# Attention to feed-forward: a residual sum earlier on VectorE, and the third pair's rows turned and split earlier

## The chip, the core and the metric

One core of a Trainium2 chip runs the whole program. Its engines are TensorE (PE in the profile; PEld is its weight load), VectorE (DVE), ScalarE (ACT), GpSimd (POOL) and SyncE (SP), each with its own list of instructions in program order, held together by semaphores. The metric is the device time of one execution in microseconds, lower is better; where a kernel has several runs, the median counts.

## What is computed

32 sequences of 128 tokens with 128 features, worked on in 16 pairs. Three blocks follow each other: attention with 16 heads, a feed-forward block, and a graph attention.

```
mod = silu(c) @ W_mod + b_mod
sh_msa, sc_msa, g_msa, sh_mlp, sc_mlp, g_mlp = split(mod, 6)
x = x + g_msa * attention(modulate(layernorm(x), sh_msa, sc_msa))
x = x + g_mlp * ff(modulate(layernorm(x), sh_mlp, sc_mlp))
x = graph_attention(x, c, adj, ...)      # uses sums over adj's last axis, plain and weighted by w_bias
```

ff is `gelu(x @ W1 + b1) @ W2 + b2` with 512 hidden features. Matmul operands are split into a high part (a cast to fp32r) and a low part (the rest), and three products are added up.

## The kernel before

Every phase is a function that writes out, for each engine, the order of its steps by hand. attention_phase walks the 16 pairs; its last pair (LAST, number 15) has a body of its own, last_body, in which the feed-forward block begins for the first pairs: `fed.` calls are steps of ffn_phase, and F0 to F3 are its first four pairs. DONE stands for the step after LAST, in which LAST's output is projected, gated, turned back and summed.

What happens for one pair of the feed-forward block, in order: moments (VectorE, mean and variance), rstd_of (GpSimd), normalise (VectorE, L1671), turn (TensorE, two transposes into PSUM, L1503), modulate (ScalarE, L1607, from PSUM to f_xT in SBUF), split (VectorE: CAST to f_xT_hi, L1685, then the difference f_xT_lo, L1687, a TENSOR_TENSOR whose two inputs lie in SBUF), hidden(F, 0) and hidden(F, 2) (TensorE, L1516 to L1518), gelu (ScalarE), output (TensorE, L1527), gate (ScalarE), turn_back (TensorE, L1536), residual (VectorE, L1695).

The end of the attention for one pair: probs_v (TensorE, L754), save_oT_high and save_oT_low (VectorE, L1119 and L1124; ScalarE L1030 for two of the last), project_out in two halves of 12 matmuls (TensorE, L777 to L779), gate (VectorE: a COPY of four columns, L1135, then two TENSOR_SCALARs, L1140), turn_back (TensorE, L787), residual (VectorE, L1152), and the store of x1 by SyncE. All of a pair's output goes through the PSUM bank "out", which is bank C; residual frees it. In LAST's body turn_p(LAST, 1, 1) is the next to write bank C (tp_o10 in the table LAST_BODY). turn_p (TensorE, L737) turns the probabilities, which GpSimd has scaled (L611).

Beside this run the sums over adj: ScalarE casts the numbers (L315), VectorE sums them (sum_cells, L319), GpSimd multiplies them by w_bias (weigh, L324), VectorE sums again. The last weigh is for pair 15 and waits for sum_cells(15), which stands in last_body's end on VectorE.

The feed-forward block's turn for F2 writes the lower half of bank 2, and project_out(DONE) the upper half of bank 3. turn(F2) waits for normalise(F2) and for modulate(F1).

Of the kernel before, what the change touches and what calls it, by code (L numbers as in the profile page):

```python
# [393 lines left out]
def attention_phase(nc, g, ctx, setup, ffn, graph, edges):  # L394
# [66 lines left out]
    def bank_of(s, name):  # L461
        return dict(uses(s.n) if isinstance(s.n, int) else BODY)[name]
# [36 lines left out]
    def wait_free(eng, s, name):  # L499

        eng.wait_ge(bank_free[bank_of(s, name)], count_to(s, name, True))

    def wait_empty(eng, s, name):

        mine = 0 if name in ("xt0", "xt", "fed") else 1
        zero_wait(eng, bank_free[bank_of(s, name)], count_to(s, name, True) - mine)

    def wait_full(eng, s, name):

        eng.wait_ge(bank_full[bank_of(s, name)], count_to(s, name, False))  # L510

    def unit_of(s, half, b):
        return s.n * 4 + (2 * half + b)
# [7 lines left out]
    def weighted_at(s, half, b):  # L521

        return (step_from(s, 1), f"pv_e{b}") if half else (s, f"pv_o{b}")
# [6 lines left out]
    LAST = Step((PAIRS - 1) // 2, (PAIRS - 1) % 2)  # L530
# [14 lines left out]
    F0, F1, F2, F3 = (Step(n // 2, n % 2) for n in range(4))  # L545
# [124 lines left out]
    def tensor(pe):  # L670
# [69 lines left out]
        def probs_v(s, half, b):  # L740

            if half:
                wait_free(pe, s, f"v1{'ab'[b]}")
            else:
                wait_free(pe, step_from(s, -1), f"v0{'ab'[b]}")
            for grp in range(2):
                wait_free(pe, s, turn_name(half, b, grp))
            at_step, name = weighted_at(s, half, b)
            wait_empty(pe, at_step, name)
            bank = bank_of(at_step, name)  # L750
            for j in range(4):
                for e in range(2):
                    head = 8 * half + 2 * j + e
                    last = pe.matmul(work_ps[bank][64 * e:64 * e + 64, j * T:j * T + T],  # L754
                                     v[:, b, head * DH:head * DH + DH], pT[b][:, 2 * j + e, :],
                                     start=True, stop=True)
            last.then_inc(bank_full[bank], 1)

        def project_out(s, half):

            bank = bank_of(s, "out")
            if half == 0:
                wait_empty(pe, s, "out")
                if at(s, 1):
                    pe.wait_ge(g.kept_loaded, KEPT * 16)
                    pe.wait_ge(w_out_split, 1)
                for b in range(2):
                    at_step, name = weighted_at(step_from(s, -1), 0, b)
                    wait_free(pe, at_step, name)
            else:  # L770
                for b in range(2):
                    at_step, name = weighted_at(step_from(s, -1), 1, b)
                    wait_free(pe, at_step, name)
            dst = work_ps[bank][:, 0:2 * T]
            for c in range(4 * half, 4 * half + 4):
                hi, lo = (t[:, c].rearrange("p b t -> p (b t)") for t in (oT_hi, oT_lo))
                pe.matmul(dst, g.w_out_hi[:, c, :], hi, start=(c == 0), stop=False)  # L777
                pe.matmul(dst, g.w_out_hi[:, c, :], lo, start=False, stop=False)  # L778
                last = pe.matmul(dst, g.w_out_lo[:, c, :], hi, start=False, stop=(c == CHUNKS - 1))  # L779
            if half:  # L780
                last.then_inc(bank_full[bank], 1)
# [79 lines left out]
        def last_body():  # L861

            prev = step_from(LAST, -1)
            fed = ffn.parts["tensor_steps"](pe)
            probs_v(prev, 1, 0)
            probs_v(prev, 1, 1)
            scores(LAST, 1, 0)
            scores(LAST, 1, 1)
            turn_p(LAST, 0, 0)
            fed.wait_split(F0)  # L870
            project_v(LAST, "v1a")
            project_v(LAST, "v1b")
            project_out(LAST, 0)
            turn_p(LAST, 0, 1)
            project_out(LAST, 1)

            pe.wait_ge(g.w1_split, 1)
            pe.wait_ge(exp_done, unit_of(LAST, 1, 0) * 8 + 8)
            fed.hidden(F0, 0)
            probs_v(LAST, 0, 0)  # L880
            probs_v(LAST, 0, 1)
            turn_back(LAST)
            pe.wait_ge(exp_done, unit_of(LAST, 1, 1) * 8 + 8)
            fed.turn(F1, fed.turn_ps(F1))
            fed.hidden(F0, 2)
            turn_p(LAST, 1, 0)
            turn_p(LAST, 1, 1)
            fed.hidden(F1, 0)
            probs_v(LAST, 1, 0)
            probs_v(LAST, 1, 1)  # L890
            fed.hidden(F1, 2)
            project_out(DONE, 0)
            project_out(DONE, 1)
            fed.turn(F2, fed.turn_ps(F2))
            fed.output(F0)
            turn_back(DONE)

# [155 lines left out]
    def vector(dve):  # L1053
# [62 lines left out]
        def save_oT_high(s, half, b):  # L1116
            at_step, name, bank, src = oT_at(s, half, b)
            wait_full(dve, at_step, name)
            dve.tensor_copy(oT_hi[:, 4 * half:4 * half + 4, b, :], src).then_inc(oT_high, 1)  # L1119

        def save_oT_low(s, half, b):
            at_step, name, bank, src = oT_at(s, half, b)
            dve.wait_ge(oT_high, unit_of(s, half, b) + 1)
            dve.tensor_tensor(oT_lo[:, 4 * half:4 * half + 4, b, :], src,  # L1124
                              oT_hi[:, 4 * half:4 * half + 4, b, :].bitcast(F32),
                              ALU.subtract).then_inc(bank_free[bank], 1)
# [6 lines left out]
        def gate(s):  # L1133

            dve.tensor_copy(gate_cols[:], pair_cols(step_from(s, -1), slice(6, 8))).then_inc(gate_cols_ready, 1)  # L1135
            dve.wait_ge(gate_cols_ready, s.n)
            wait_full(dve, s, "out")
            src = work_ps[bank_of(s, "out")]
            for b in range(2):
                last = dve.tensor_scalar(gatedT[:, b, :], src[:, b * T:b * T + T], gate_cols[:, b, 0:1],  # L1140
                                         gate_cols[:, b, 1:2], ALU.mult, ALU.add)
            last.then_inc(gated, 1)

        def residual(s):

            dve.wait_ge(residual_loaded, s.n * 16)
            if not at(s, 1):
                dve.wait_ge(x1_stored, (s.n - 1) * 16)
            dve.wait_ge(turned_back, s.n)
            bank = bank_of(s, "out")  # L1150
            flat = lambda t: t[:].rearrange("p b f -> p (b f)")
            dve.tensor_tensor(flat(x1), work_ps[bank][:, 2 * T:4 * T], flat(x_res),  # L1152
                              ALU.add).then_inc(bank_free[bank], 1)
# [95 lines left out]
        def last_body():  # L1249

            prev = step_from(LAST, -1)
            fed = ffn.parts["vector_steps"](dve)
            save_oT_high(prev, 1, 0)
            save_oT_low(prev, 1, 0)
            save_oT_high(prev, 1, 1)
            invert_sums(LAST, 0, 1)
            row_max(LAST, 1, 0)
            save_oT_low(prev, 1, 1)
            save_turned(LAST, 0, 0)
            row_max(LAST, 1, 1)  # L1260
            fed.moments(F1)
            edges.parts["sum_labels"](dve, PAIRS - 2)
            save_turned(LAST, 0, 1)
            invert_sums(LAST, 1, 0)
            gate(LAST)
            fed.normalise(F1)
            fed.copy_mod_cols(F1)
            invert_sums(LAST, 1, 1)
            save_oT_high(LAST, 0, 0)
            save_oT_low(LAST, 0, 0)  # L1270
            save_oT_high(LAST, 0, 1)
            save_oT_low(LAST, 0, 1)
            residual(LAST)
            fed.split(F1)
            save_turned(LAST, 1, 0)
            save_turned(LAST, 1, 1)
            fed.moments(F2)
            fed.copy_mod_cols(F2)
            save_oT_low(LAST, 1, 0)
            save_oT_low(LAST, 1, 1)  # L1280
            fed.normalise(F2)
            fed.moments(F3)
            fed.copy_gate_cols(F0)
            edges.parts["sum_cells"](dve, PAIRS - 1)
            gate(DONE)
            fed.split(F2)
            residual(DONE)
            fed.normalise(F3)

# [36 lines left out]
def step_from(s, k):  # L1326

    return Step(s.half + (s.par + k) // 2, (s.par + k) % 2)
# [7 lines left out]
def at(s, n):  # L1336

    return isinstance(s.n, int) and s.n == n
# [1230 lines left out]
```

## Time and profile before

| what | value |
|---|---|
| median of 3 runs | 591.07 us (590.46 to 592.23) |
| the profiled execution's own time | 591.09 us |
| its span | 589.5 us |
| TensorE busy | 579.8 us, 98% |
| VectorE busy | 508.2 us, 86% |
| ScalarE busy | 474.7 us, 81% |
| GpSimd busy | 294.0 us, 50% |
| granted TensorE clock | 1.00 (2.4 GHz) |

Busy shares are means over the three blocks. last_body runs from about 371 to 397 us of the span, and the steps that are moved lie between 382 and 396 us. Times in the rows are microseconds from the span's start; a row that joins several instructions has their count behind an x and their joint duration. The number in square brackets is idle time of the engine in front of the row, with what released it. Ends of matmuls are modelled.

### The profile page before, as it was taken

The page shows a single profiled execution, that of the slowest core. Times are in us where ns is not written, and L with a number is a line of the kernel's source. Part 1 is how long each engine was busy: PE and PEld are TensorE (multiplying, and loading weights), DVE is VectorE, ACT ScalarE, POOL GpSimd, SP SyncE. Part 2 cuts the span into 40 slices and gives each one's busy share as a digit, 9 for nine tenths or more (in the row PEclk, how much of TensorE's full clock was granted, in tenths as well). Part 3 has the DMA queues.
Part 4 walks back from the last instruction along what each step waited for, and adds up shares of the span by engine and source line. Part 5 has one row for each costly group of instructions (what it writes and reads, how often), then busy time and mean ns, then how long its engine had stood idle before and what let it go on. Part 6 is the DMA issues. An engine that isn't in the chain of part 4 may idle for free.

```text
span 589.5 us, 17417 instructions
## 1 busy us (share of the span) xinstructions
PE 579.8 (98%) x5600; PEld 534.8 (91%) x5600; DVE 508.2 (86%) x1113; ACT 474.7 (81%) x1733; POOL 294.0 (50%) x355
## 2 busy tenths in 40 slices
PE   8999999999999999999999999999999999999997
PEld 8899899999999999999999999988988899999996
DVE  5899988998998889889888988888886989888886
ACT  4988889789879888897898798977887777777772
POOL 4547435445364355363543543646654565555652
PEclk9999999999999999999999999999999999999999
DMA  8310210211202102102012041023343433444321
GB/s 253 79 42 8 53 44 18 58 32 26 57 0 57 48 9 57 38 19 57 10 47 57 0 108 48 14 72 100 114 144 95 112 104 99 120 117 108 98 73 50
DMA packets 63428, 38.99 MB, mean 66 GB/s; under 512 B 19630, under 2 KB 61214, under 8 KB 63390
## 3 DMA queue, kind: packets, MB, share of 16 engines
q1 hardware_dynamic: 61614, 34.28, 21.9%
q0 software_dynamic: 1632, 4.21, 2.3%
q8 instruction: 21, 0.34, 0.2%
q14 instruction: 17, 0.14, 0.1%
q10 hardware_dynamic: 144, 0.02, 0.0%
HBM read 30.73 MB, written 7.76 MB: 65 GB/s over the span
## 4 chain that ended last, share of the span: by engine, by line
PE 91%; DVE 5%; ACT 2%; issue 1%; DMA 0%; POOL 0%; DVEq 0%; ACTq 0%; POOLq 0%
PE banks L724 10%; PE banks L754 10%; PE banks L737 9%; PE banks L2161 7%; PE banks L692 5%; PE banks L696 5%; PE banks L693 5%; PE banks L2129 4%; PE banks L1527 4%; PE banks L2143 4%; PE banks L777 3%; PE banks L778 2%; PE banks L779 2%; PE banks L708 2%; PE banks L710 2%; PE banks L709 2%
## 5 line engine op out<-in xcount | busy, mean ns | idle before, releaser
L611 POOL TENSOR_TENSOR late_blocks<-late_blocks,p_rsum 128x512 f32<-128x512 f32 x96 | 99.0, 1052 | 158.1 <-DVE p_rsum L1101 158.1
L951 ACT ACTIVATE late_blocks<-banks,neg_max 128x128 f32<-128x128 f32 x384 | 137.3, 404 | 27.8 <-DVE neg_max L1095 27.8
L951 ACT ACTIVATION_READ_ACCUMULATOR late_blocks<-banks,neg_max 128x1 f32 x384 | 94.0, 245 | 0.0
L932 ACT ACTIVATE wide<-banks 128x512 f32<-128x512 f32 x124 | 75.5, 611 | 5.7 <-PE banks L696 4.7
L1095 DVE TENSOR_REDUCE neg_max<-banks 128x8 f32<-128x1024 f32 x64 | 76.6, 1196 | 2.4 <-PE banks L724 2.4
L692 PE MATMUL banks<-xT_hi,w_qkv_hi 128*128 128x256 f32 x256 | 77.4, 302 | 0.0
L696 PE MATMUL banks<-xT_hi,w_qkv_lo 128*128 128x256 f32 x256 | 71.7, 280 | 0.0
L693 PE MATMUL banks<-xT_lo,w_qkv_hi 128*128 128x256 f32 x256 | 71.5, 279 | 0.0
L724 PE MATMUL banks<-wide 64*128 64x128 f32 x1024 | 66.0, 278 | 0.2
L724 PEld LDWEIGHTS banks<-wide 64*128 64x128 f32 x1024 | 59.7, 188 | 6.1 <-issue 3.7
L951 ACT ACTIVATE third_p<-banks,neg_max 128x128 f32<-128x128 f32 x128 | 46.9, 387 | 20.5 <-DVE neg_max L1095 20.5
L1119 DVE CAST oT_hi<-banks 128x512 fp32r<-128x512 f32 x62 | 42.5, 685 | 10.7 <-PE banks L754 10.5
L737 PE MATMUL banks<-ident,late_blocks 128*128 128x128 f32 x384 | 50.7, 275 | 0.9 <-DVE x L1152 0.6
L692 PEld LDWEIGHTS banks<-xT_hi,w_qkv_hi 128*128 128x128 f32 x256 | 48.4, 189 | 1.1
L693 PEld LDWEIGHTS banks<-xT_lo,w_qkv_hi 128*128 128x128 f32 x256 | 48.5, 190 | 0.6
L696 PEld LDWEIGHTS banks<-xT_hi,w_qkv_lo 128*128 128x128 f32 x256 | 48.2, 188 | 0.0
L2161 PEld LDWEIGHTS banks<-g_v_block,g_wT 120*128 120x128 f32 (+1 forms) x384 | 45.4, 191 | 2.7 <-issue 2.7
L2013 POOL TENSOR_TENSOR late_blocks<-blockmask,g_kT 128x320 f32<-128x320 f32 x32 | 27.2, 869 | 41.2 <-ACT g_kT L2244 41.2
L737 PEld LDWEIGHTS banks<-ident,late_blocks 128*128 128x128 f32 x384 | 42.9, 141 | 5.3 <-issue 0.8
L2161 PE MATMUL banks<-g_v_block,g_wT 120*128 120x54 f32 (+1 forms) x384 | 47.3, 273 | 0.0
L1124 DVE TENSOR_TENSOR oT_lo<-banks,oT_hi 128x512 fp32r<-128x512 f32 x64 | 44.0, 687 | 2.3 <-ACT oT_hi L1030 1.2
L777 PE MATMUL banks<-oT_hi,w_out_hi 128*128 128x256 f32 x128 | 36.3, 284 | 0.0
(188 smaller groups left out, 1700.3 us busy)
## 6 DMA issues: line engine op xcount, KB each, us to landing
g_v_block<-v_image SPq DMA_DIRECT2D x16, 303.8 KB, 3.5
early<-in_mask SPq DMA_DIRECT2D x16, 220.0 KB
early<-in_mask SPq DMA_DIRECT2D x80, 44.0 KB
x_in<-in_x SPq DMA_DIRECT2D x16, 128.0 KB, 2.1
x_res<-in_x SPq DMA_DIRECT2D x16, 128.0 KB, 2.2
x_scratch<-x SPq DMA_DIRECT2D x16, 128.0 KB, 1.9
f_x_in<-x_scratch SPq DMA_DIRECT2D x16, 128.0 KB, 2.4
f_x_res<-x_scratch POOLq DMA_DIRECT2D x16, 128.0 KB, 2.7
```

What stands on the lines that cost most here:

```text
L611: pool.tensor_tensor(p[:, heads, :], p[:, heads, :], p_rsum[:, b, heads].unsqueeze(2).broadcast_to([128, 4, T]), ALU.mult).then_inc(p_read ...
L692: pe.matmul(dst, g.wq_hi[:, cols], xT_hi[par][:], start=True, stop=False)
L693: pe.matmul(dst, g.wq_hi[:, cols], xT_lo[par][:], start=False, stop=False)
L696: last = pe.matmul(dst, g.wq_lo[:, cols], xT_hi[par][:], start=False, stop=True)
L724: last = pe.matmul(s_ps[b][:, e, j, :], qk[rows, c, 0, b, :], qk[rows, c, 1, b, :], start=True, stop=True)
L737: last = pe.transpose(work_ps[bank][:, m * T:m * T + T], p[:, 4 * grp + m, :], g.ident[:])
L754: last = pe.matmul(work_ps[bank][64 * e:64 * e + 64, j * T:j * T + T], v[:, b, head * DH:head * DH + DH], pT[b][:, 2 * j + e, :], start=Tr ...
L777: pe.matmul(dst, g.w_out_hi[:, c, :], hi, start=(c == 0), stop=False)
L932: act.activation(qk_dst(name) if name[0] == "q" else v_dst(name), work_ps[bank], ACT.Copy).then_inc(bank_free[bank], 1)
L951: act.activation(p[:, m, :], s_ps[b][:, e, j, :], ACT.Exp, bias=neg_max[:, b, 4 * e + j:4 * e + j + 1], accum_out=p_sum[:, b, m:m + 1]).th ...
L1095: dve.tensor_reduce(out=neg_max[:, b, :].rearrange("p (e j) -> p e j", e=2), in_=s_ps[b], op=ALU.max, axis=AX.X, negate=True).then_inc(max ...
L2161: last = pe.matmul(out_ps[:, d, heads, :], wT[0:rows, d, c, :], v_block[0:rows, s.par, b, 0:rows // NG, d, c, :], start=True, stop=True)
```

## The change

On TensorE, turn(F2) goes from behind project_out(DONE) to between its halves. On VectorE, residual(LAST) goes ahead of save_oT_high and save_oT_low(LAST, 0, 1), and split(F2) goes ahead of gate(DONE). No instruction is added or removed.

```
@@ tensor, last_body
             fed.hidden(F1, 2)
             project_out(DONE, 0)
+            fed.turn(F2, fed.turn_ps(F2))
             project_out(DONE, 1)
-            fed.turn(F2, fed.turn_ps(F2))
             fed.output(F0)
             turn_back(DONE)
@@ vector, last_body
             save_oT_high(LAST, 0, 0)
             save_oT_low(LAST, 0, 0)
+            residual(LAST)
             save_oT_high(LAST, 0, 1)
             save_oT_low(LAST, 0, 1)
-            residual(LAST)
             fed.split(F1)
@@ vector, last_body
             edges.parts["sum_cells"](dve, PAIRS - 1)
+            fed.split(F2)
             gate(DONE)
-            fed.split(F2)
             residual(DONE)
             fed.normalise(F3)
```

## Rows read from the trace of the kernel before

**Rows 1.** The page, part 4: the chain that ended last, shares by engine

```profile
PE 91%; DVE 5%; ACT 2%; issue 1%; DMA 0%; POOL 0%; DVEq 0%; ACTq 0%; POOLq 0%
```

**Rows 2.** The chain in order of time, 376 to 406 us: start, us, what

```profile
384.24 0.42 DVE x L1152
...
394.24 0.44 DVE f_xT_lo L1687
```

**Rows 3.** Timeline of TensorE: start, us, instruction, count [idle before, releaser]

```profile
381.96 0.44 PE L787 MATMUL banks<-ident,gatedT 128*128 128x128 f32 x2
...
384.80 1.06 PE L737 MATMUL banks<-ident,late_blocks 128*128 128x128 f32 x8 [0.60 <-DVE x L1152]
385.62 0.36 PE L1516 MATMUL banks<-f_xT_hi,w_hi 128*128 128x256 f32 x1
...
389.22 0.29 PE L777 MATMUL banks<-oT_hi,w_out_hi 128*128 128x256 f32 x1
...
392.10 0.38 PE L1503 MATMUL banks<-ident,f_xhat 128*128 128x128 f32 x2
...
394.05 0.38 PE L787 MATMUL banks<-ident,gatedT 128*128 128x128 f32 x2
394.72 0.39 PE L1516 MATMUL banks<-f_xT_hi,w_hi 128*128 128x256 f32 x1 [0.29 <-DVE f_xT_lo L1687]
...
395.57 0.44 PE L1503 MATMUL banks<-ident,f_xhat 128*128 128x128 f32 x2
...
396.54 0.38 PE L1536 MATMUL banks<-ident,f_gatedT 128*128 128x128 f32 x2
```

**Rows 4.** Timeline of ScalarE, 376 to 408 us

```profile
392.57 0.81 ACT L1607 ACTIVATE f_xT<-banks,f_mod_cols 128x128 f32<-128x128 f32 x2 [1.90 <-issue]
```

**Rows 5.** Timeline of VectorE, 376 to 408 us

```profile
382.92 0.68 DVE L1119 CAST oT_hi<-banks 128x512 fp32r<-128x512 f32 x1
...
384.89 0.42 DVE L1687 TENSOR_TENSOR f_xT_lo<-f_xT,f_xT_hi 128x256 fp32r<-128x256 f32 x1
...
389.76 0.60 DVE L1671 TENSOR_SCALAR f_xhat<-f_x_in,f_meanvar,f_rstd 128x128 f32<-128x128 f32 x2
...
391.00 1.06 DVE L319 TENSOR_REDUCE edge_sums<-early 128x80 f32<-128x880 f32 x1
391.98 0.16 DVE L1135 COPY gate_cols<-modT 128x4 f32<-128x4 f32 x1
392.37 0.73 DVE L1140 TENSOR_SCALAR gatedT<-banks,gate_cols 128x128 f32<-128x128 f32 x2 [0.23 <-PE banks L779]
393.40 0.80 DVE L1685 CAST f_xT_hi<-f_xT 128x256 fp32r<-128x256 f32 x1 [0.30 <-ACT f_xT L1607]
...
394.59 0.42 DVE L1152 TENSOR_TENSOR x<-banks,x_res 128x256 f32<-128x256 f32 x1
394.92 0.59 DVE L1671 TENSOR_SCALAR f_xhat<-f_x_in,f_meanvar,f_rstd 128x128 f32<-128x128 f32 x2
...
397.03 0.42 DVE L1695 TENSOR_TENSOR f_x<-banks,f_x_res 128x256 f32<-128x256 f32 x1 [0.70 <-PE banks L1536]
```

**Rows 6.** The instructions of L1685: duration ns min/median/max, first and last start

```profile
L1685 DVE CAST f_xT_hi<-f_xT x15: 282/294/804, 384.6 to 442.2; 128x256 fp32r<-128x256 f32 x15
```

**Rows 7.** Timeline of GpSimd, 376 to 420 us: the last weigh

```profile
392.14 1.92 POOL L324 TENSOR_TENSOR early<-early,w_bias_sb 128x880 f32<-128x880 f32 x1
```

**Rows 8.** Timeline of VectorE, 355 to 360 us and 40.8 to 42.2 us

```profile
355.92 1.29 DVE L1671 TENSOR_SCALAR f_xhat<-f_x_in,f_meanvar,f_rstd 128x128 f32<-128x128 f32 x2
357.13 1.03 DVE L1677 COPY f_mod_cols<-modT 128x16 f32<-128x16 f32 x1
...
40.91 1.17 DVE L1130 TENSOR_TENSOR w_out_lo<-late_outputs,w_out_hi 128x1024 fp32r<-128x1024 f32 x1
```

**Rows 9.** Timeline of GpSimd in the same two stretches

```profile
356.09 2.04 POOL L611 TENSOR_TENSOR third_p<-third_p,p_rsum 128x512 f32<-128x512 f32 x2 [0.84 <-DVE p_rsum L1101]
...
41.08 1.91 POOL L611 TENSOR_TENSOR late_blocks<-late_blocks,p_rsum 128x512 f32<-128x512 f32 x1 [5.91 <-DVE p_rsum L1101]
```

More of the change, by code:

```diff
@@ L892, in last_body @@
             project_out(DONE, 0)
+            fed.turn(F2, fed.turn_ps(F2))
             project_out(DONE, 1)
-            fed.turn(F2, fed.turn_ps(F2))
             fed.output(F0)
@@ L1270, in last_body @@
             save_oT_low(LAST, 0, 0)
+            residual(LAST)
             save_oT_high(LAST, 0, 1)
             save_oT_low(LAST, 0, 1)
-            residual(LAST)
             fed.split(F1)
@@ L1284, in last_body @@
             edges.parts["sum_cells"](dve, PAIRS - 1)
+            fed.split(F2)
             gate(DONE)
-            fed.split(F2)
             residual(DONE)
```

## Prediction

> **What bounds the kernel now.** I read the chain of work that ended last first: 91% of it is TensorE [rows 1]. So a microsecond is won or lost only where TensorE waits, or where a wait is made. The window 376 to 406 us of the chain and TensorE's timeline show the two waits that this change aims at. The first is 0.60 us in front of turn_p(LAST,1,1) at 384.80, released by the residual sum that ends at 384.66 [rows 2, 3]: bank C is the "out" bank, and residual(LAST) frees it. The second is 0.29 us in front of hidden(F2,0) at 394.72, released by the low half of split(F2), which ends at 394.67 [rows 2, 3]. Two things made that split late: modulate(F2) starts only at 392.57, because the turn it reads starts at 392.10, behind all 24 matmuls of the projection [rows 3, 4]; and the split's CAST took 0.80 us, where the middle one of 15 takes 0.294 [rows 5, 6].
>
> **Part 1, residual(LAST) in front of save_oT_high/low(LAST,0,1).** VectorE's instructions are the same, only in another order. residual needs turn_back(LAST), which is over at 381.96 + 0.44 = 382.40 [rows 3], and its two DMA conditions are of older steps. It takes the place of the CAST at 382.92 and ends at 382.92 + 0.42 = 383.34 [rows 2, 5]. TensorE is free at 384.80 - 0.60 = 384.20 and then turns at once. What is late next is hidden(F1,0), which began at 385.62 right behind the turn: it needs split(F1), which stays where it was, because the same work lies ahead of it, and ends at 384.89 + 0.42 = 385.31 [rows 3, 5]. With 0.05 us from VectorE to TensorE (394.24 + 0.43 = 394.67 to 394.72) it starts at 385.36. So of the 0.60 us, s = 385.62 - 385.36 = **0.26 us** are won. Behind the split the rest can't be had. save_oT_low(LAST,0,1) ends 0.4 later, and frees a bank that probs_v(LAST,1,1) writes next, which comes after hidden(F1,0). SyncE's store of x1 and its next loads go out 1.3 us sooner; nobody waits for them here. Bounds of s: 0 (if TensorE found another wait) to 0.60; I take 0.26, which two rows give.
>
> **Part 2, turn(F2) between the halves of project_out(DONE).** TensorE issues the same instructions. The 24 matmuls run from 389.22 to 392.10, 0.12 each, so half of them end at 389.22 - 0.26 + 1.44 = 390.40. The turn's input is ready at 389.76 + 0.60 - 0.26 = 390.10 [rows 3, 5], so it doesn't wait; 0.3 us are to spare. If they were gone, the projection's second half, behind it on TensorE, would be late by what is missing. The turn is over at 390.40 + 0.38 = 390.78, and ScalarE, which is through with its gelu by then (it stood idle for 1.90 us before 392.57), starts modulate(F2) 0.09 later (392.48 to 392.57) and ends at 390.87 + 0.81 = **391.68** [rows 3, 4]. The projection and the turn together take what they took, so the projection is through when the turn was before, less s, and gate(DONE) finds it about when it did.
>
> **Part 3, split(F2) in front of gate(DONE).** Here it goes wrong. VectorE's sum over cells starts at 391.00 - 0.26 = 390.74, and the instruction behind it 0.98 later (391.00 to 391.98), at 391.72 [rows 5]. That is now split(F2)'s CAST, whose input has been there since 391.68. GpSimd's weigh, 128x880, starts at 392.14 - 0.26 = 391.88 [rows 7]. The two engines exclude each other in this trace. A COPY of 16 columns at 357.13 took 1.03 us and ended with GpSimd's pair of multiplies (356.09 + 2.04 = 358.13); two 128x128 TENSOR_SCALARs just before took 1.29, where such a pair takes 0.60, so GpSimd slips in between two VectorE instructions [rows 8, 9]. The CAST at 393.40 is a case of the same: it ended at 394.20, 0.14 after weigh's 394.06 [rows 5, 7]. For TENSOR_TENSOR with both inputs in SBUF, which is split(F2)'s second half, the trace has the other order only: one of 1.17 us started at 40.91 and ended at 42.08, and GpSimd's multiply, begun at 41.08, took 1.91, where one of the pair at 356.09 takes 1.02 [rows 8, 9]. So it holds what GpSimd wants, and I take it that it also waits for it. The bounds of its cost are 0.42 (free) and all of weigh plus 0.28.
> The Trainium skill (SBUF — State Buffer, section Who interferes with whom) says just that: a VectorE instruction with two SBUF inputs contends with a GpSimd one that reads SBUF, and whichever issues first keeps the port pair to its end. The trace agrees for the order it shows; by the rule the forecast below stands, and without it rival (c) would be likelier than it is put here.
> Step by step: the CAST holds from 391.72 to 392.01. weigh gets in behind it; the delayed multiply at 41.08 ended 0.91 after VectorE's end, 0.11 less than its own 1.02, so weigh ends at 392.01 + 1.92 - 0.11 = 393.82, hardly later than undelayed (391.88 + 1.92 = 393.80, which I take). The low half is held until then and ends 0.14 + (0.43 - 0.29) = 0.28 later, at 394.08. gate(DONE) now stands behind it: its COPY starts 0.08 ahead of that end (394.59 against 394.67), its multiplies 0.16 later (391.98 to 392.37, less the wait of 0.23), and they take 0.73: 394.00 + 0.16 + 0.73 = 394.89 [rows 2, 5]. TensorE has issued output(F0) and stands before turn_back(DONE) since 394.05 - 0.26 = 393.79; it goes on at 394.94 [rows 3]. This is the new wait, some 1.15 us. residual(DONE) follows a turn's start by 0.49 (396.54 to 397.03), normalise(F3) follows that by 0.33 and takes 0.59, and turn(F3) follows its end by 0.06 [rows 3, 5]: 394.94 + 0.49 + 0.33 + 0.59 + 0.06 = **396.41**, where it was 395.57. hidden(F2,0), in between, needs 0.85 (394.72 to 395.57) and fits.
> From turn(F3) on every engine follows TensorE, so the shift of **+0.84 us** is kept to the end: 591.09 (profiled execution, span 589.5) + 0.84 = 591.93. The median of the runs shown, 591.07, is 0.02 below the profiled time, so the forecast is **591.9**.
>
> **Rivals.** (a) GpSimd is first. The CAST beats weigh by 0.16 us only; if modulate(F2) or anything ahead of it is later by more, the CAST itself is held until 393.80, ends 0.14 after it, and the low half takes another 0.47: 394.41, so +0.33 on the forecast, +1.17 in all, 592.3. For it: the short margin. Against: both start from the same sum over cells.
> (b) The low half isn't held (ends 392.48), but the 4-column COPY in gate(DONE) is, like the 16-column one at 357.13. It ends with weigh, gate ends about 0.29 sooner than in the forecast: +0.55, 591.6.
> (c) The other side: neither is held. Then the gate is done at 392.40 + 0.16 + 0.73 = 393.29, before TensorE comes to turn_back(DONE) at 393.79; residual(DONE), normalise(F3) and turn(F3) follow at 393.79 + 0.49 + 0.33 + 0.59 + 0.06 = 395.26: 0.31 us faster, 590.8. It decides at the end of the split: up to about 392.9 the gate is in time. More than 0.31 can't be had, because normalise(F3) stands behind residual(DONE), which needs turn_back(DONE); the 0.6 us won at hidden(F2,0) are given back there. Against it: 357.13 and 41.08.
> (d) Part 1 gives nothing (s = 0), the rest as forecast: +1.10, 592.2.
>
> **How the numbers follow.** Forecast 0.47, (a) 0.22, (b) 0.10, (c) 0.13, (d) 0.03, something else 0.05. The cases slower than before hold 0.82, from 591.6 to 592.3; with (c) at 590.8 they hold 0.95. A median of runs lies up to half a microsecond beside its kernel's profile (the three runs of before span 590.46 to 592.23), so the range is 590.7 to 592.8. About 0.3%, 1.8 us, is what a measurement of this kernel can tell from no change: every case is within it. Slower by more needs (a) and 0.6 us on top, 0.10; faster by more has no case here and gets 0.03; the rest, 0.87, is within.
>
> **What would show it.** Part 1: turn_p(LAST,1,1) starts near 384.2 and the wait before hidden(F1,0) names split(F1). Part 2: turn(F2) lies between two sets of 12 matmuls with no wait, and modulate(F2) starts near 390.9. Part 3: the CAST of split(F2) takes 0.29 and its TENSOR_TENSOR about 2.0 us, ending with weigh (the forecast); or the CAST about 2.2 (a); or the COPY of the gate about 1.4 (b); or none (c). TensorE has its longest wait of this stretch before turn_back(DONE), released by gatedT. The prediction is wrong if turn(F3) comes before 395.6, if TensorE's later stretches don't keep the shift, or if the turn between the halves waits for its input.

## The result, and the profile after

| | before | changed |
|---|---|---|
| median | 591.40 us (590.27 to 592.23, 15 runs) | 592.52 us (591.33 to 592.86, 15 runs) |
| ratio | 1 | 1.0019, 95% interval 1.0012 to 1.0026 |
| span of the profiled execution | 589.5 us | 591.0 us |

The changed kernel is slower by 0.19%, about 1.1 us, and the interval lies clear of 1. The two spans differ by 1.5 us, but 0.52 of it is there before any changed instruction runs: VectorE's first score maximum starts at 14.25 in one and 14.77 in the other, in identical code. So all comparisons of traces below go by distances within a trace. The yardstick is D, from the start of turn_back(LAST) (L787, 381.96 in rows 3), which no part of the change moves, to the start of turn(F3) (L1503, 395.57), behind which every engine follows TensorE. D was 13.61 us before and is 397.11 - 382.49 = **14.62** in the changed kernel, 1.01 us more.

Timeline of TensorE, changed kernel (start, us, instruction, count, idle before and its releaser); the rows answer to [rows 3]:

```profile
382.49 0.44 PE L787 MATMUL banks<-ident,gatedT 128*128 128x128 f32 x2
...
384.56 1.04 PE L737 MATMUL banks<-ident,late_blocks 128*128 128x128 f32 x8
385.89 0.39 PE L1516 MATMUL banks<-f_xT_hi,w_hi 128*128 128x256 f32 x1 [0.29 <-DVE f_xT_lo L1687]
...
390.96 0.38 PE L1503 MATMUL banks<-ident,f_xhat 128*128 128x128 f32 x2
...
395.54 0.44 PE L787 MATMUL banks<-ident,gatedT 128*128 128x128 f32 x2 [1.04 <-DVE gatedT L1140]
...
397.11 0.44 PE L1503 MATMUL banks<-ident,f_xhat 128*128 128x128 f32 x2 [0.42 <-DVE f_xhat L1671]
```

The wait of 0.60 us in front of L737 is gone, and one of 0.29 stands behind it, in front of hidden(F1,0). The turn for F2 has no wait. Two more are new: 1.04 us in front of turn_back(DONE), for the gate, and 0.42 in front of turn(F3). The profile counts a wait from the modelled end of the matmuls; from start to start turn_back(DONE) comes 2.93 us behind output(F0), 392.61 to 395.54, where it was 1.73, 392.32 to 394.05.

Timeline of VectorE, changed kernel, and under it GpSimd's weigh; they answer to [rows 5] and [rows 7]:

```profile
391.30 1.07 DVE L319 TENSOR_REDUCE edge_sums<-early 128x80 f32<-128x880 f32 x1
392.28 0.29 DVE L1685 CAST f_xT_hi<-f_xT 128x256 fp32r<-128x256 f32 x1
392.60 2.04 DVE L1687 TENSOR_TENSOR f_xT_lo<-f_xT,f_xT_hi 128x256 fp32r<-128x256 f32 x1
394.56 0.15 DVE L1135 COPY gate_cols<-modT 128x4 f32<-128x4 f32 x1
394.75 0.73 DVE L1140 TENSOR_SCALAR gatedT<-banks,gate_cols 128x128 f32<-128x128 f32 x2
396.11 0.42 DVE L1152 TENSOR_TENSOR x<-banks,x_res 128x256 f32<-128x256 f32 x1 [0.63 <-PE banks L787]
396.45 0.60 DVE L1671 TENSOR_SCALAR f_xhat<-f_x_in,f_meanvar,f_rstd 128x128 f32<-128x128 f32 x2
```

```profile
392.44 1.91 POOL L324 TENSOR_TENSOR early<-early,w_bias_sb 128x880 f32<-128x880 f32 x1
```

The CAST starts 0.16 us ahead of weigh and takes its plain 0.29; the low half of the split takes 2.04 and ends 0.29 behind weigh's 394.35. No wait is printed for it: VectorE counts as busy. What gives it away is the spread of the line, whose 15 instructions have this least, middle and longest duration in ns:

```profile
L1687 DVE TENSOR_TENSOR f_xT_lo<-f_xT,f_xT_hi x15: 424/426/2039, 385.4 to 444.0; 128x256 fp32r<-128x256 f32 x15
```

In the chain of work the same stretch appears as time in which nothing was waited for that the profile shows:

```profile
392.60 0.24 DVE f_xT_lo L1687
392.84 1.73 issue
394.56 0.17 DVE gate_cols L1135
...
395.54 0.45 PE banks L787 x2
```

The shift is kept to the end. The last sum of the program, first before and then changed:

```profile
587.18 0.29 DVE L2378 SCALAR_TENSOR_TENSOR g_y<-g_y,g_x_res 128x128 f32<-128x128 f32 x1
```

```profile
588.70 0.29 DVE L2378 SCALAR_TENSOR_TENSOR g_y<-g_y,g_x_res 128x128 f32<-128x128 f32 x1
```

588.70 - 587.18 = 1.52 is 0.53, the start, plus 0.99, where the stretch has 1.01.

### The profile page after: what moved, and what is told of

Same layout as the page of the kernel before. It is cut to its first block, busy times and chain, and to the rows that moved or that the text cites. A ratio compares the mean times of both kernels' runs of the same rounds, so it can differ in the third digit from the quotient of the medians.

```text
span 591.0 us, 17417 instructions
## 1 busy us (share of the span) xinstructions
PE 580.6 (98%) x5600; PEld 535.3 (91%) x5600; DVE 509.1 (86%) x1113; ACT 474.5 (80%) x1733; POOL 294.0 (50%) x355
## 4 chain that ended last, share of the span: by engine, by line
PE 91%; DVE 5%; ACT 2%; issue 1%; DMA 0%; POOL 0%; DVEq 0%; ACTq 0%; POOLq 0%
PE banks L724 10%; PE banks L754 10%; PE banks L737 9%; PE banks L2161 7%; PE banks L692 5%; PE banks L696 5%; PE banks L693 5%; PE banks L2129 4%; PE banks L1527 4%; PE banks L2143 4%; PE banks L777 2%; PE banks L779 2%; PE banks L778 2%; PE banks L708 2%; PE banks L709 2%; PE banks L710 2%
## 5 line engine op out<-in xcount | busy, mean ns | idle before, releaser
L737 PE MATMUL banks<-ident,late_blocks 128*128 128x128 f32 x384 | 50.7, 275 | 0.3 <-DVE late_weights L1108 0.3
L737 PEld LDWEIGHTS banks<-ident,late_blocks 128*128 128x128 f32 x384 | 42.9, 141 | 4.5 <-POOL late_blocks L611 0.5
```

The costliest lines, as they stand in the source:

```text
L737: last = pe.transpose(work_ps[bank][:, m * T:m * T + T], p[:, 4 * grp + m, :], g.ident[:])
```

## The experiments

The theory: VectorE's TENSOR_TENSOR with two SBUF inputs and GpSimd's multiply exclude each other (the lock theory in the expectations), and what is queued behind the held one on VectorE pays. Lock is the theory's name for it: what the traces show is which instruction is long, and that it ends with GpSimd's. The main rival: it is the order of split and gate, or the turn between the halves, that costs. D and the whole time for each run. Each ratio is to the kernel before measured beside it (591.40 for the changed kernel), and need not be the quotient of the two medians:

| kernel | D, us | low half of split(F2), us | median and ratio to before, 95% interval |
|---|---|---|---|
| before | 13.61 | 0.43 | 591.27 or 591.20 beside the experiments |
| changed | 14.62 | 2.04 | 592.52, 1.0019 (1.0012 to 1.0026) |
| part 1 alone | 13.39 | 0.42 | 591.24, 1.0001 (0.9992 to 1.0010) |
| parts 1 and 2 | 13.39 | 0.42 | 590.83, 0.9991 (0.9982 to 1.0000) |
| part 3 alone | 15.14 | 0.43 | 593.31, one run |
| changed, light weigh | 13.36 | 0.42 | 590.99, 0.9993 (0.9984 to 1.0003) |
| changed, weigh waits | 13.36 | 0.42 | 590.65, 0.9992 (0.9983 to 1.0001) |
| changed, split reads PSUM | 14.27 | 0.42 | 591.84, one run |
| changed, weigh waits, normalise(F3) first | 12.91 | 0.42 | 590.15, 0.9986 (0.9977 to 0.9995) |
| changed, two weighs | 16.56 | 2.03 | 595.46, one run |

**Part 1 alone.**

```
+            residual(LAST)
             save_oT_high(LAST, 0, 1)
             save_oT_low(LAST, 0, 1)
-            residual(LAST)
```

> Before with part 1 alone: residual(LAST) ahead of save_oT_high and save_oT_low(LAST,0,1). I measure the stretch D from the start of turn_back(LAST), L787, which no part moves, to the start of turn(F3), L1503: 13.61 us in the kernel before, 14.62 in the changed one. My theory: the win of 0.26 in front of hidden(F1,0) goes through the whole stretch, D = 13.35 to 13.40, median 0.2 to 0.3 us below before. The rival (the later wait at hidden(F2,0) swallows it, because weigh, and with it the CAST held by it, does not move): D = 13.6, no change.

D is 395.36 - 381.97 = 13.39, as expected: 0.22 us are won, and they go through the stretch, since weigh, the CAST held by it and everything else come sooner alike. But the median isn't 0.2 to 0.3 below before, as expected: it is 0.03 below, and the last sum of this trace starts at 587.19, where that of before does. The win is lost again at 411 us, in a wait of VectorE for an input load, which the kernel before doesn't have there; TensorE's turn that started 0.19 sooner than before at 410.63 is followed by one only 0.01 sooner at 414.40.

```profile
410.84 0.49 DVE L1661 BATCH_NORM_STATS2 f_stats<-f_x_in 128x6 f32<-128x128 f32 x2 [0.33 <-DMA f_x_in<-x_scratch]
```

The load was issued 0.20 us sooner too (407.13, before 407.33), but took 3.7 us to land instead of 3.4. In the runs with parts 1 and 2, with the light weigh and with the weigh behind the split, whose D is as short, the same load took 2.1 or 2.2 us, VectorE has no such wait, and the last sum keeps the win. So it is a slower load in the execution profiled, not a price of the sooner work; why it was slower, and whether it happens in others of the 11 runs, is open. The ratio of 1.0001 doesn't tell 0 from -0.2 us.

**Parts 1 and 2.**

```
             project_out(DONE, 0)
+            fed.turn(F2, fed.turn_ps(F2))
             project_out(DONE, 1)
-            fed.turn(F2, fed.turn_ps(F2))
```

> Parts 1 and 2, without part 3: turn(F2) between the halves, but split(F2) behind gate(DONE). Lock theory: the CAST now reaches VectorE at about 0.35 us earlier than before but is still held until weigh ends, so it takes about 0.9 us where it is 0.29 alone, and turn_back(DONE) is in time; D = 13.35 to 13.45, no better than part 1 alone, median 0.2 to 0.3 us below before. Rival, that the loss of the changed kernel comes from the turn between the halves: D stays above 14.

```profile
392.43 0.73 DVE L1140 TENSOR_SCALAR gatedT<-banks,gate_cols 128x128 f32<-128x128 f32 x2 [0.45 <-PE banks L779]
393.07 0.98 DVE L1685 CAST f_xT_hi<-f_xT 128x256 fp32r<-128x256 f32 x1
394.09 0.42 DVE L1687 TENSOR_TENSOR f_xT_lo<-f_xT,f_xT_hi 128x256 fp32r<-128x256 f32 x1
```

D is 395.41 - 382.02 = 13.39, the same as with part 1 alone. The CAST, which no longer waits for ScalarE, starts sooner in its frame and takes 0.98 instead of 0.80: it ends 0.14 us after weigh either way (weigh: 391.99 and 1.92 long). By D, part 2 on top of part 1 costs nothing and gives nothing; the medians are too close to tell the two apart.

**Part 3 alone.**

```
+            fed.split(F2)
             gate(DONE)
-            fed.split(F2)
```

> Part 3 alone: split(F2) ahead of gate(DONE), with turn(F2) behind the projection and residual(LAST) late, as before. Lock theory: the CAST starts and ends where it did (0.80 us, held by weigh), the low half is free (0.43), gate(DONE) comes behind them and turn_back(DONE) about 1.45 us later than before; D = 15.0 to 15.1. Order theory without a lock (the low half takes 2 us wherever it stands ahead of the gate): D above 16.

```profile
393.91 0.80 DVE L1685 CAST f_xT_hi<-f_xT 128x256 fp32r<-128x256 f32 x1 [1.34 <-ACT f_xT L1607]
394.74 0.43 DVE L1687 TENSOR_TENSOR f_xT_lo<-f_xT,f_xT_hi 128x256 fp32r<-128x256 f32 x1
395.09 0.16 DVE L1135 COPY gate_cols<-modT 128x4 f32<-128x4 f32 x1
```

D is 397.63 - 382.49 = 15.14, a little over the 15.0 to 15.1 expected. Here the low half stands ahead of the gate too, and takes 0.43, because the CAST in front of it was already held to weigh's end. So the 2.04 us go with weigh's place in time, not with the order on VectorE. The cost in this kernel is another: VectorE, with the gate behind it, waits 1.34 us for modulate(F2), which part 2 would have brought forward, then the held CAST takes 0.80, and TensorE waits 1.36 for the gate.

**The changed kernel with a light weigh** (pair 15's label sums are not weighted, but for 11 of 880 columns).

```
+        if isinstance(i, int) and i == PAIRS - 1:
+            pool.tensor_tensor(val[:, 0:1], val[:, 0:1], g.w_bias[:].unsqueeze(1).broadcast_to([128, 1, L]),
+                               ALU.mult).then_inc(cells_weighted, 1)
+            return
```

> The changed kernel with GpSimd's last weigh cut from 880 columns to 11: the label sums of pair 15's tokens are then not multiplied by w_bias, which is left out here. Lock theory: the TENSOR_TENSOR of split(F2) takes 0.42 instead of 2.04 us, turn_back(DONE) does not wait, D = 13.3 to 13.4, median 0.2 to 0.3 us below before. Rival (the order of split and gate costs it whatever GpSimd does): 2.04 us and D = 14.6 as in the changed kernel.

```profile
392.26 0.28 DVE L1689 CAST f_xT_hi<-f_xT 128x256 fp32r<-128x256 f32 x1
392.57 0.42 DVE L1691 TENSOR_TENSOR f_xT_lo<-f_xT,f_xT_hi 128x256 fp32r<-128x256 f32 x1
392.92 0.16 DVE L1139 COPY gate_cols<-modT 128x4 f32<-128x4 f32 x1
393.12 0.73 DVE L1144 TENSOR_SCALAR gatedT<-banks,gate_cols 128x128 f32<-128x128 f32 x2
394.81 0.42 DVE L1156 TENSOR_TENSOR x<-banks,x_res 128x256 f32<-128x256 f32 x1 [0.97 <-PE banks L791]
```

```profile
392.42 0.22 POOL L325 TENSOR_TENSOR early<-early,w_bias_sb 128x11 f32<-128x11 f32 x1
```

```profile
394.29 0.38 PE L791 MATMUL banks<-ident,gatedT 128*128 128x128 f32 x2
395.81 0.44 PE L1507 MATMUL banks<-ident,f_xhat 128*128 128x128 f32 x2 [0.45 <-DVE f_xhat L1675]
```

VectorE's order is that of the changed kernel and the low half takes 0.42. D is 395.81 - 382.45 = 13.36, 1.26 below the changed kernel: all of its loss, and the win of part 1 on top. VectorE now waits 0.97 us for turn_back(DONE), so what ends the stretch is turn_back(DONE), residual(DONE), normalise(F3).

**The changed kernel, weigh behind the split.**

```
+            begin.wait_split = lambda s: pool.wait_ge(xT_split, s.n * 2 + 2)
...
             fed.rstd_of(F3)
+            fed.wait_split(F2)
             edges.parts["weigh"](pool, PAIRS - 1)
```

> The changed kernel, whole, with one wait more: GpSimd's last weigh starts only when split(F2) is done. Lock theory: the low half takes 0.42 us, the COPY of the gate starts 0.15 us before weigh can, turn_back(DONE) does not wait, D (turn_back(LAST) to turn(F3), 14.62 in the changed kernel, 13.36 with the light weigh) = 13.35 to 13.45; weigh itself starts about 0.65 us later, and nobody needs it for 6 us. Median about 0.25 us below before and 1.2 us below the changed kernel. Rival: the moved weigh meets another VectorE step (the COPY of the gate, or normalise(F3)) and costs the same there, D = 14.3 or more.

```profile
391.98 0.42 DVE L1689 TENSOR_TENSOR f_xT_lo<-f_xT,f_xT_hi 128x256 fp32r<-128x256 f32 x1
392.32 0.16 DVE L1136 COPY gate_cols<-modT 128x4 f32<-128x4 f32 x1
```

```profile
392.48 1.92 POOL L324 TENSOR_TENSOR early<-early,w_bias_sb 128x880 f32<-128x880 f32 x1 [0.70 <-DVE f_xT_lo L1689]
```

D is 395.23 - 381.87 = 13.36, as with the light weigh, with the whole of weigh done. The multiply is the same and as long; only who comes first is changed. The COPY is 0.16 us ahead of it.

**The changed kernel, the split reads PSUM.**

```
+                dst = turn_ps(s)[:, b * T:b * T + T] if at(s, 2) else xT[:, b, :]
-                last = act.activation(xT[:, b, :], turn_ps(s)[:, b * T:b * T + T], ACT.Identity,
+                last = act.activation(dst, turn_ps(s)[:, b * T:b * T + T], ACT.Identity,
...
-            flat = xT[:].rearrange("p b t -> p (b t)")
+            flat = turn_ps(s) if at(s, 2) else xT[:].rearrange("p b t -> p (b t)")
```

> The changed kernel, weigh untouched, but ScalarE's modulate(F2) writes its result back to the PSUM bank that it reads, and split(F2) reads it there: its TENSOR_TENSOR then has one SBUF input. By the rule of two SBUF inputs it takes 0.42 us in the middle of weigh, and its CAST 0.42. The next in line is the 4-column COPY of the gate, SBUF to SBUF: if it is held as I suppose (my rival b), it takes 1.2 to 1.4 us, ends with weigh, and D = 14.2 to 14.35. If so small a COPY is not held, D = 13.4 to 13.5. If the low half is held whatever it reads: 2 us again and D = 14.6.

```profile
391.86 0.41 DVE L1686 CAST f_xT_hi<-banks 128x256 fp32r<-128x256 f32 x1
392.31 0.42 DVE L1688 TENSOR_TENSOR f_xT_lo<-banks,f_xT_hi 128x256 fp32r<-128x256 f32 x1
392.65 1.31 DVE L1135 COPY gate_cols<-modT 128x4 f32<-128x4 f32 x1
393.99 0.73 DVE L1140 TENSOR_SCALAR gatedT<-banks,gate_cols 128x128 f32<-128x128 f32 x2
```

```profile
392.02 1.91 POOL L324 TENSOR_TENSOR early<-early,w_bias_sb 128x880 f32<-128x880 f32 x1
```

With one input in PSUM the low half runs in the middle of weigh, at its plain 0.42. (The CAST starts 0.16 ahead of weigh, so it tells nothing of being held.) The COPY behind them, SBUF to SBUF and 4 columns wide, is held: 1.31 us, to 393.96, where weigh ends at 393.93. D is 396.34 - 382.07 = 14.27. So one input in PSUM is enough to free the TENSOR_TENSOR, and even a COPY of 4 columns is held when both its sides are in SBUF. The kernel before shows the same of an instruction with its one large input in PSUM: the gate's two TENSOR_SCALARs, begun 0.23 us into weigh, took 0.73 [rows 5, 7], as they do with the light weigh.

**The changed kernel, two weighs** (pair 15's label sums are weighted twice).

```
+        if isinstance(i, int) and i == PAIRS - 1:
+            pool.tensor_tensor(val, val, g.w_bias[:].unsqueeze(1).broadcast_to([128, CELLS, L]),
+                               ALU.mult).then_inc(weigh_doubled, 1)
+            pool.wait_ge(weigh_doubled, 1)
```

> The changed kernel with the last weigh run twice, one behind the other, both 1.9 us (pair 15's label sums are then weighted twice, a change of what is computed). Lock theory with the order of arrival: the low half, waiting since before the first weigh's end, gets in between the two and takes 2.04 us as before; the 4-column COPY of the gate then meets the second weigh and is held until its end, so D = 14.62 + 1.75 = 16.3 to 16.6. If so small a COPY is not held: D = 14.6 to 14.8. If GpSimd keeps the port over both: the low half takes about 4 us and D = 16.5.

```profile
392.87 2.03 DVE L1692 TENSOR_TENSOR f_xT_lo<-f_xT,f_xT_hi 128x256 fp32r<-128x256 f32 x1
394.82 1.88 DVE L1140 COPY gate_cols<-modT 128x4 f32<-128x4 f32 x1
396.74 0.73 DVE L1145 TENSOR_SCALAR gatedT<-banks,gate_cols 128x128 f32<-128x128 f32 x2
```

```profile
392.71 1.91 POOL L326 TENSOR_TENSOR early<-early,w_bias_sb 128x880 f32<-128x880 f32 x1
394.70 1.98 POOL L329 TENSOR_TENSOR early<-early,w_bias_sb 128x880 f32<-128x880 f32 x1
```

The engines take turns, in the order in which they come: CAST, first weigh, low half, second weigh, COPY. The second weigh starts while the low half runs and takes 0.07 more than the first. D is 399.34 - 382.78 = 16.56. The expectation gave 16.5 also for a GpSimd that keeps VectorE out over both; it is the low half's 2.03, not 4, that speaks against it. Of the 1.94 over the changed kernel's 14.62, 1.69 is there at turn_back(DONE), 397.52 - 382.78 = 14.74 against 13.05, and goes with the COPY's 1.88 instead of 0.15. The other 0.25 is TensorE's clock, told in the last section: the residual starts 0.83 behind turn_back (398.35) instead of 0.57.

**The changed kernel, weigh behind normalise(F3), and that ahead of the gate.**

```
             fed.split(F2)
+            fed.normalise(F3)
             gate(DONE)
             residual(DONE)
-            fed.normalise(F3)
...
+            begin.wait_normalised = lambda s: pool.wait_ge(xhat_ready, s.n * 2 + 2)
...
             fed.rstd_of(F3)
+            fed.wait_normalised(F3)
             edges.parts["weigh"](pool, PAIRS - 1)
...
+    g.wait_last_out = lambda eng: wait_free(eng, DONE, "out")
...
             turn_back(step_from(s, -2))
+            if at(s, 2):
+                g.wait_last_out(pe)
             output(step_from(s, -1))
```

The last two are needed because output(F1) writes the PSUM bank that residual(DONE) reads, and TensorE's wait for normalise(F3) had ordered them until then.

> The changed kernel with normalise(F3) between split(F2) and gate(DONE), weigh waiting for normalise(F3), and output(F1) waiting for residual(DONE), which nothing else orders then. With the lock out of the way, what ends the stretch is turn_back(DONE), residual(DONE), normalise(F3), one behind the other; this takes the last two off it. The gate is then done about 0.1 us after TensorE comes to turn_back(DONE), and turn(F3) follows hidden(F2,0) without a wait: D = 12.9 to 13.05, median 0.6 to 0.7 us below before. Rival: the gate, 0.5 us later on VectorE, or weigh, 1.2 us later, is late next, and D stays above 13.3.

```profile
392.39 0.42 DVE L1693 TENSOR_TENSOR f_xT_lo<-f_xT,f_xT_hi 128x256 fp32r<-128x256 f32 x1
392.73 0.60 DVE L1677 TENSOR_SCALAR f_xhat<-f_x_in,f_meanvar,f_rstd 128x128 f32<-128x128 f32 x2
393.25 0.16 DVE L1136 COPY gate_cols<-modT 128x4 f32<-128x4 f32 x1
393.44 0.73 DVE L1141 TENSOR_SCALAR gatedT<-banks,gate_cols 128x128 f32<-128x128 f32 x2
```

```profile
393.41 1.93 POOL L324 TENSOR_TENSOR early<-early,w_bias_sb 128x880 f32<-128x880 f32 x1 [1.21 <-DVE f_xhat L1677]
```

```profile
395.22 0.38 PE L1507 MATMUL banks<-ident,f_xhat 128*128 128x128 f32 x2
```

D is 395.22 - 382.31 = 12.91, 0.70 below before, and turn(F3) has no wait. The median is 590.15 beside 591.20 of before, ratio 0.9986 (0.9977 to 0.9995): 1.05 us by the medians and 0.8 by the ratio, a little more than the 0.6 to 0.7 expected. It is the only kernel here whose interval lies wholly below 1; it beats before, and the changed kernel, whose interval lies above 1, by more.

## Why the prediction was right

The case that was given the best chance, 0.47, came true in each of its steps. The time alone doesn't show that: 592.52 lies nearer to the 592.3 of rival (a) than to the forecast's 591.9. The traces do, by their steps. Their times, with the changed trace's 0.53 us taken off:

| step | forecast | measured |
|---|---|---|
| hidden(F1,0) starts | 385.36 | 385.36 |
| turn(F2) starts | 390.40 | 390.43 |
| modulate(F2) starts | 390.87 | 390.90 |
| CAST of split(F2) starts | 391.72, 0.29 long | 391.75, 0.29 long |
| weigh starts | 391.88 | 391.91 |
| low half ends | 394.08 | 394.11 |
| gate(DONE) ends | 394.89 | 394.95 |
| turn_back(DONE) starts | 394.94 | 395.01 |
| turn(F3) starts | 396.41 | 396.58 |

*Part 1* was sized at 0.26 us and gave 0.22 alone. Half the difference is TensorE's restart: from the first matmul of hidden(F1,0) to the second it is 0.22 behind the wait (385.39 to 385.61), 0.20 before. The other half is there already when it starts. One step was misread without harm: turn_p(LAST,1,1) was to start at 384.20, the end of the matmuls ahead of it as modelled, and started at 384.03 (384.56 less 0.53); hidden(F1,0) waits for the split all the same.

*Part 2* has no wait, as forecast, and parts 1 and 2 together give no more than part 1. The forecast said why nothing could be had there: the stretch ends at turn_back(DONE), residual(DONE) and normalise(F3). The run with the light weigh shows it, where the split is done 1.3 us before TensorE comes to turn_back(DONE) and D is still 13.36; the run with normalise(F3) taken out of that row wins 0.45 more.

*Part 3* is the whole loss. Its open step was whether the low half waits for GpSimd, which the kernel before showed only the other way round [rows 8, 9]. It does: 2.04 us against 0.42 with a light or later weigh. The rule of the Trainium skill on which the forecast leant (SBUF — State Buffer, section Who interferes with whom) says that a VectorE instruction with two SBUF inputs contends with GpSimd's reads, and that one with at most one doesn't, outside the modes that use both ports. For TENSOR_TENSOR the runs agree with both clauses: 2.04 us with two, 0.42 with one. The COPY with its single SBUF input was held all the same (1.31 us), so it would have to fall under the exception; no run here shows in which mode it ran.

*The size.* The step gave +0.84 us, the traces show +1.01, the medians +1.1 (interval 0.7 to 1.5). The term that was mis-sized most is the last one: I took 0.49 us from turn_back's start to residual's, from a turn back of the feed-forward block that TensorE reached in its stride, and it was 0.57 (395.54 to 396.11) behind a wait. The runs with the light weigh and with the weigh behind the split have this very pair in stride, at 0.52 (394.29 to 394.81, 393.72 to 394.24): so 0.05 go with the wait, behind which the two transposes take 0.44 instead of 0.38, and 0.03 with the row, which was of another step. The steps from residual(DONE) to turn(F3) add 0.02. 0.03 lie in the gate's COPY (0.19 to the multiplies, not 0.16), 0.03 in the restart of part 1, and 0.01 between the gate and TensorE. The forecast time of 591.9 was low by 0.6: 0.3 of it is the median of before, 591.07 in the three runs shown and 591.40 in fifteen, about 0.2 the stretch, and 0.1 the difference between medians and traces.

*The rivals.* (a), GpSimd first at the CAST, didn't happen here: the CAST was 0.16 us ahead, as forecast. It is what the run with parts 1 and 2 shows, a CAST of 0.98 us. (b), the small COPY, was true as a mechanism and hidden as a price: the low half covers it, and the run with the split out of PSUM uncovers it, D = 14.27 where its sum (+0.55, so 14.16) stood close. (c) is the run with the weigh behind the split: -0.25 where -0.31 was forecast.

## What to carry to other kernels

On VectorE, look at what GpSimd is doing at the time to which a step is moved: a copy, cast or scalar operation from SBUF to SBUF, or a TENSOR_TENSOR with two SBUF inputs, can last until GpSimd's multiply ends (here 1.88 us for 0.15, 0.98 for 0.29, 1.29 for 0.60 and 2.04 for 0.42), and everything behind it in VectorE's order pays, though the profile prints no wait. Here it was better to leave the split behind the gate, which TensorE needed next (D 13.39), or to hold GpSimd's step, which was in no hurry, behind it with a semaphore (D 13.36). And before a wait is shortened, follow the row of dependent steps to where the engines meet again; here a second row (turn back, residual, normalise) ended within 0.05 us of the one that was shortened: turn_back(DONE) at 394.05 and 0.49 more is 394.54, and residual(DONE) started at 394.59 [rows 3, 5].

## What the runs showed that I had not expected

A wait on TensorE can cost more than its length. With two weighs it waited 2.75 us for the gate, and its granted clock fell to half, 1.2 GHz, for about 3 us, after TensorE had run without a gap up to the end of output(F0) at 394.77 and then stood still; with the 1.04 us of the changed kernel and the 1.36 of part 3 alone it stayed at 1.00. The columns are the stretch, its length, the busy times (and counts) of TensorE, its weight load, VectorE, ScalarE and GpSimd, then the clock as a share of 2.4 GHz, the DMA share and GB/s:

```profile
394.00:397.00 3.00, 0.77 (x4) 0.34 (x2) 2.96 (x3) 0.81 (x2) 2.59 (x2) 1.00 0.00 1
397.00:398.00 1.00, 0.48 (x3) 0.48 (x3) 0.46 (x2) 0.00 (x0) 0.00 (x0) 0.56 0.00 0
398.00:399.00 1.00, 1.00 (x6) 1.00 (x6) 0.66 (x3) 0.00 (x0) 0.00 (x0) 0.50 0.00 0
399.00:400.00 1.00, 1.00 (x6) 0.86 (x5) 0.96 (x9) 0.47 (x2) 0.00 (x0) 0.50 0.27 80
400.00:402.00 2.00, 2.00 (x14) 1.90 (x13) 0.72 (x4) 1.90 (x6) 0.88 (x2) 0.87 0.33 91
```

The two transposes of turn_back(DONE) took 0.69 us there and 0.44 in the changed kernel. By the next turn, F4's at 403.50, this kernel is 403.50 - 382.78 = 20.72 us from turn_back(LAST), where before it was 399.17 - 381.96 = 17.21: 3.51 us more, of which D, at turn(F3), had shown 2.95.

The other surprise is small: a single profiled execution can hide a win. Part 1 alone won 0.22 us and lost it 16 us later to a load that took 3.7 us to land, where three other runs with the same stretch took 2.1 or 2.2.
